# Attention's input x turned by VectorE and moved by DMA; output tiles 2 and 3 re-placed

## What is computed

```python
x = x + jnp.tanh(g_xattn[0]) * _L0_xattn_ref(_layernorm(x, axis=-1), ctx_1024, ctx_1024, mask_BxS2_if1, Wq, bq, ...)
x = x + jnp.tanh(g_ffn[0]) * _L0_ffn_ref(_layernorm(x, axis=-1), W_r, W_k, W_v, mu_r, mu_k)
```

## Time and profile before

| | |
|---|---|
| median of the runs | 1876.82 us |
| the profiled execution | 1877.37 us |
| its span | 1875.6 us, granted clock 0.996 |
| TensorE busy | 1843.8 us, 98% |
| VectorE / ScalarE / GpSimd busy | 1372.9 / 1069.8 / 1142.2 us |
| DMA, mean | 130 GB/s, 243.32 MB |

### The profile page before, as it was taken

One profiled execution on the slowest core, in us unless ns is written; L12 is line 12 of the kernel. 1 busy time (PEld: TensorE's weight loads), 2 busy tenths in 40 slices (PEclk: granted clock), 3 DMA queues, 4 the chain that ended last, 5 costly groups with the idle time before them and its releaser, 6 DMA issues.

```text
span 1875.6 us, 35183 instructions
## 1 busy us (share of the span) xinstructions
PE 1843.8 (98%) x10928; PEld 1449.0 (77%) x10928; DVE 1372.9 (73%) x3732; ACT 1069.8 (57%) x2055; POOL 1142.2 (61%) x1833
## 2 busy tenths in 40 slices
PE   6999999999999999999999999999999999999999
PEld 5677777777777777777777777777678888888887
DVE  6776777677676777677677677767688787888864
ACT  5655555565555556555565555556575555656562
POOL 2777777777677777767777777776652423233231
PEclk9999999999999999999999999999999999999999
DMA  7555465445546545554645556465244535353421
GB/s 220 105 133 129 125 159 122 129 122 143 132 113 163 124 119 127 143 148 100 163 114 124 134 130 156 114 159 141 68 135 124 146 108 162 100 149 112 140 86 68
DMA packets 159801, 243.32 MB, mean 130 GB/s; under 512 B 22752, under 2 KB 51424, under 8 KB 158848
## 3 DMA queue, kind: packets, MB, share of 16 engines
q1 hardware_dynamic: 159616, 241.07, 49.7%
HBM read 92.06 MB, written 33.59 MB: 67 GB/s over the span
## 4 chain that ended last, share of the span: by engine, by line
PE 94%; DVE 3%; issue 1%; DMA 1%; POOL 0%; ACT 0%; SPq 0%; DVEq 0%; ACTq 0%
PE proj_ps L41 15%; PE proj_ps L42 15%; PE proj_ps L43 15%; PE score_ps L1446 10%; PE prob_ps L1470 8%; PE value_ps L1489 8%; PE score_ps L41 3%; PE score_ps L43 3%; PE score_ps L42 3%; PE sum_ps L1497 2%; PE sum_ps L43 1%; PE sum_ps L41 1%; PE sum_ps L42 1%; PE value_ps L41 1%; PE value_ps L43 1%; PE value_ps L42 1%
## 5 line engine op out<-in xcount | busy, mean ns | idle before, releaser
L1089 DVE CUSTOM_DVE_ANT_0 score_ps<-score_ps,causal 128x128 f32<-128x128 f32 (+3 forms) x1024 | 488.8, 505 | 291.5 <-PE score_ps L1446 291.4
L692 ACT ACTIVATE probs<-prob_ps 128x512 f32<-128x512 f32 (+1 forms) x768 | 396.1, 528 | 368.6 <-PE prob_ps L1470 184.6
L1446 PE MATMUL score_ps<-k_stack,q_stack 97*128 97x128 f32 (+3 forms) x1024 | 318.9, 353 | 4.5 <-DVE least L1089 3.6
L1470 PE MATMUL prob_ps<-q_stack,k_stack 100*128 100x512 f32 (+3 forms) x1024 | 280.5, 314 | 2.8 <-DMA q_stack<-max_rows 2.7
L563 POOL TENSOR_TENSOR kact<-square,kact 128x512 fp32r<-128x512 f32 x64 | 96.0, 1510 | 306.3 <-ACT kact L778 306.3
L495 POOL TENSOR_TENSOR prob_sum<-probs 128x384 f32<-128x384 f32 x256 | 260.0, 1016 | 0.0
L1446 PEld LDWEIGHTS score_ps<-k_stack,q_stack 97*128 97x128 f32 x1024 | 187.5, 189 | 75.1 <-issue 39.8
L498 POOL TENSOR_TENSOR prob_sum<-prob_sum,probs 128x256 f32<-128x256 f32 x256 | 198.2, 774 | 37.0 <-POOL prob_sum L495 0.4
L1470 PEld LDWEIGHTS prob_ps<-q_stack,k_stack 100*128 100x128 f32 x1024 | 192.0, 191 | 22.3 <-DMA q_stack<-max_rows 3.3
L484 POOL TENSOR_SCALAR_AFFINE_SELECT probs<-probs 128x256 f32<-128x256 f32 x256 | 104.7, 409 | 152.7 <-ACT probs L692 152.7
L488 POOL TENSOR_SCALAR_AFFINE_SELECT probs<-probs 128x256 f32<-128x256 f32 x256 | 106.8, 417 | 125.1 <-ACT probs L692 125.1
(11 more groups left out here) (180 smaller groups left out, 4665.2 us busy)
## 6 DMA issues: line engine op xcount, KB each, us to landing
k_stack<-staged SPq DMA_DIRECT2D x384, 128.0 KB
q_stack<-staged SPq DMA_DIRECT2D x384, 128.0 KB, 3.1
x_io<-in_x SPq DMA_DIRECT2D x16, 1024.0 KB, 7.9
x<-x_io SPq DMA_DIRECT2D x64, 256.0 KB, 3.1
res<-x SPq DMA_DIRECT2D x64, 256.0 KB, 3.4
out_x<-res SPq DMA_DIRECT2D x64, 256.0 KB, 5.4
tiles<-in_x SPq DMA_DIRECT2D x15, 1024.0 KB, 5.4
tiles<-in_ctxT SPq DMA_DIRECT2D x60, 256.0 KB, 3.9
```

Source lines behind the costliest of these rows:

```text
L692: nc.scalar.activation(probs[:, u % RING, lo:hi], prob_ps[(3 * u + c) % 2][:, 0:hi - lo], ACT.Exp, scale=SCALE).then_inc(exp_done, 1)
L1089: nc.vector.tensor_tensor_reduce(out=here, in0=here, in1=causal[:, LATE - P * t:S], scale=-1.0, scalar=3e38, op0=ALU.add, op1=ALU.min, acc ...
L1446: last = nc.tensor.matmul(here[:, at:at + P * (t + 1)], q_stack[n][0:MASK_ROW + 1, j, P * t:P * t + P], k_stack[n][0:MASK_ROW + 1, j, 0:P ...
L1470: last = nc.tensor.matmul(here[:, at:at + width], k_stack[n][0:ROWS, j, P * k:P * k + P], q_stack[n][0:ROWS, j, P * k:S], start=True, stop ...
```

## The change

For the batches 1 to 15 the x is no longer transposed on TensorE. The new room `turning` holds per tile 128 + 512 columns; `tiles` is its upper 512. Step by step for batch b+1:

- `load_x` makes four DMAs of 32 partitions, so that partition 32a+c, tile m holds token 128a+32m+c.
- `apply_layernorm` writes 128 columns lower, and within each chunk with features regrouped (the write goes in steps of 32 elements).
- Slot 8, between `maximum` 1 and 2, VectorE: four `turn_normalised`, one per chunk, each a transposition in 32x32 blocks of 128x512, each waiting for the one before.
- Slot 9, SyncE: `move_normalised` 0 and 1 ahead of `stack_q`, 2 and 3 behind it, each 256 KB from 32 partitions of `tiles` into all 128 partitions of x_room[1] (the room of xT_low). They wait for the turned tiles and for the last queries of batch b.
- Slots 10 and 11: `high_part_x` and `low_part_x` in their old places, but both now read x_room[1] in SBUF, not a bank.
- xT is kept by quarters of 128 tokens; the queries' moving operand is read as 4 pieces of 128 columns.
- `load_c` waits for the four moves.

Output tiles 2 and 3 start in the first place of slots 10 and 11, one chunk there, two in the second place, one in the third; tile 2 goes to the queries' bank 0. x_io has 3 tiles: tile 2 shares the room of tile 0, so its residual is loaded in slot 8 after tile 0 is stored, and its bias is added by GpSimd in slot 10, not in slot 3. The residual comes in four DMAs. For the last batch tile 2 uses `turning`. The x of the FFN's first batch is still transposed on TensorE in slots 10 and 11 of batch 15, with tiles 0 and 2 now in the keys' bank, so that `x0` waits for `k_low`. `x_blocks` of the FFN moves to another room.

The diff, cut to its changed lines; conditions that keep the old way for batch 0, and semaphores, are left out:

```diff
-        tiles = sb("tiles", [P, T, D])
-        x_io = sb("x_io", [P, T, D])
+        turning = sb("turning", [P, T, P + D])
+        tiles = turning[:, :, P:P + D]
+        x_io = sb("x_io", [P, 3, D])
...
-            10: ("x0+,x1+", "o2- 01", "o2- 23,x2+"),
-            11: ("x3+", "o3- 01", "o3- 23"),
+            10: ("x0+,x1+,o2- 0", "o2- 12", "o2- 3,x2+"),
+            11: ("x3+,o3- 0", "o3- 12", "o3- 3"),
...
-                "q3": 0, "k3": 1, "x0": 0, "x1": 2, "x2": 0, "x3": 2, "o2": 1, "o3": 1}
+                "q3": 0, "k3": 1, "x0": 0, "x1": 2, "x2": 0, "x3": 2, "o2": 0, "o3": 1}
...
-                  "q3": ("o0", -1), "x0": ("q3", -1), "x2": ("x0", 0), "x3": ("x1", 0),
+                  "q3": ("o0", -1), "o2": ("q3", 1), "x0": ("o2", -2), "x2": ("x0", 0), "x3": ("x1", 0),
...
-                  "k3": ("o1", -1), "o2": ("k3", 1), "o3": ("o2", 0)}
+                  "k3": ("o1", -1), "o3": ("k3", 1)}
...
+        def x_bank(b, m):
+            return proj_ps[1] if b == B and m % 2 == 0 else bank(f"x{m}")
...
-                if 0 <= b < B:
+                if 0 <= b < B and (name[0] != "x" or b == 0):
...
-        x_blocks = x_io[:].rearrange("p t d -> p (t d)").rearrange("p (n m c) -> p n m c", m=T, c=SIDE)
+        x_blocks = wo_room[1][:].rearrange("p t d -> p (t d)").rearrange("p (n m c) -> p n m c", m=T, c=SIDE)
...
+        def x_row(b, m):
+            return turning[:, :, 0:P] if (b, m) == (B - 1, 2) else x_io[:, (0, 1, 0, 2)[m], :]
...
+        def as_row(here, b, m):
+            return here.rearrange("p (n c) -> p n c", n=T) if (b, m) == (B - 1, 2) else here
...
+        def quarter(tensor, a):
+            return tensor[:].rearrange("p k n -> p (k n)")[:, K * P * a:K * P * a + K * P]
...
+        def by_quarters(tensor, k):
+            return tensor[:].rearrange("p k n -> p (k n)").rearrange("p (a k n) -> p a k n", a=QUARTERS, k=K)[:, :, k, :]
...
+        def turned_on_tensor(b):
+            return T * (0 if b == 0 else b - B + 1)
...
-                    sp.wait_ge(xt_done, T * b)
+                    sp.wait_ge(xt_done, turned_on_tensor(b))
...
-                    sp.wait_ge(xt_done, T * (b - 1))
+                    sp.wait_ge(xt_done, turned_on_tensor(b - 1))
...
+                elif b < B:
+                    for a in range(QUARTERS):
+                        here = x[b, P * a:P * a + P].rearrange("(m c) d -> c m d", c=SIDE)
+                        sp.dma_start(tiles[SIDE * a:SIDE * a + SIDE], here).then_inc(x_loaded, 16)
...
-                    here = (x[b] if b < B else x1[b - B]).rearrange("(t p) d -> p t d", p=P)
-                    sp.dma_start(tiles[:] if b <= B else x_in[:], here).then_inc(x_loaded, 16)
+                    here = x1[b - B].rearrange("(t p) d -> p t d", p=P)
+                    sp.dma_start(tiles if b <= B else x_in[:], here).then_inc(x_loaded, 16)
...
+            def move_normalised(b, a):
+                sp.wait_ge(ln_turned, K * b)
+                sp.wait_ge(q_done, K * b)
+                sp.dma_start(quarter(x_room[1], a), tiles[SIDE * a:SIDE * a + SIDE]).then_inc(ln_moved[a], 16)
...
-                sp.wait_ge(xt_done, T * b + k + 1)
+                for a in range(QUARTERS):
+                    sp.wait_ge(ln_moved[a], 16 * b)
...
-            def load_residual(b):
-                for m in range(T if b > 0 else 0):
-                    sp.wait_ge(x1_stored[m], 16 * b)
-                sp.dma_start(x_io[:], x[b].rearrange("(t p) d -> p t d", p=P)).then_inc(res_loaded, 16)
+            def load_residual(b, m):
+                if m == 2 and b < B - 1:
+                    sp.wait_ge(x1_stored[0], 16 * (b + 1))
+                elif m == 2:
+                    for n in range(QUARTERS):
+                        sp.wait_ge(ln_moved[n], 16 * (B - 1))
+                elif b > 0:
+                    sp.wait_ge(x1_stored[2 if m == 0 else m], 16 * b)
+                elif m < 2:
+                    sp.wait_ge(mask_stored, 16)
+                sp.dma_start(x_row(b, m), as_row(x[b, P * m:P * m + P], b, m)).then_inc(res_loaded[m], 16)
...
-                sp.dma_start(x1[b, P * m:P * m + P], x_io[:, m, :]).then_inc(x1_stored[m], 16)
+                sp.dma_start(as_row(x1[b, P * m:P * m + P], b, m), x_row(b, m)).then_inc(x1_stored[m], 16)
...
-                    load_residual(b - 1)
+                    for m in (0, 1, 3):
+                        load_residual(b - 1, m)
+                    if b == B:
+                        load_residual(b - 1, 2)
+                if has_prev and s == 8:
+                    load_residual(b - 1, 2)
+                if has_next and s == 9:
+                    move_normalised(b + 1, 0)
+                    move_normalised(b + 1, 1)
...
+                if has_next and s == 9:
+                    move_normalised(b + 1, 2)
+                    move_normalised(b + 1, 3)
...
-                pool.wait_ge(res_loaded, 16 * (b + 1))
-                nc.gpsimd.tensor_tensor(x_io[:, m, :], x_io[:, m, :], bo_gated[:], ALU.add).then_inc(res_ready, 1)
+                pool.wait_ge(res_loaded[m], 16 * (b + 1))
+                nc.gpsimd.tensor_tensor(x_row(b, m), x_row(b, m), as_row(bo_gated[:], b, m), ALU.add).then_inc(res_ready, 1)
...
-                if s in (2, 3) and 0 <= b - 1 < B - 1:
-                    add_residual_bias(b - 1, 2 * (s - 2))
-                    add_residual_bias(b - 1, 2 * (s - 2) + 1)
+                if s == 2 and 0 <= b - 1 < B - 1:
+                    add_residual_bias(b - 1, 0)
+                    add_residual_bias(b - 1, 1)
+                if s == 3 and 0 <= b - 1 < B - 1:
+                    add_residual_bias(b - 1, 3)
+                if s == 10 and 0 <= b - 1 < B - 1:
+                    add_residual_bias(b - 1, 2)
...
-                here = x_tile(b, m)
-                nc.scalar.activation(here, here, ACT.Identity, bias=newton[:, 3, m:m + 1], scale=newton[:, 1, m:m + 1]
+                here = there = x_tile(b, m)
+                if 0 < b < B:
+                    here = here.rearrange("p (k c g) -> p k c g", k=K, g=QUARTERS)
+                    there = turning[:, m, 0:D].rearrange("p (k g c) -> p k c g", k=K, g=QUARTERS)
+                nc.scalar.activation(there, here, ACT.Identity, bias=newton[:, 3, m:m + 1], scale=newton[:, 1, m:m + 1]
...
-                act.wait_ge(xt_done, T * b + m + 1)
-                if b > 0:
+                if b == 0:
+                    act.wait_ge(xt_done, m + 1)
+                    nc.scalar.copy(quarter(xT[0], m), bank(f"x{m}")[:]).then_inc(xt_high, 1)
+                else:
+                    act.wait_ge(ln_moved[m], 16 * b)
...
-                nc.scalar.copy(xT[0][:, :, P * m:P * m + P], bank(f"x{m}")[:].rearrange("p (k n) -> p k n", k=K)
-                               ).then_inc(xt_high, 1)
+                    nc.scalar.copy(quarter(xT[0], m), quarter(x_room[1], m)).then_inc(xt_high, 1)
...
-                act.wait_ge(xt_done, T * (B + j) + m + 1)
+                act.wait_ge(xt_done, turned_on_tensor(B + j) + m + 1)
...
-                here = bank(f"x{m}") if j == 0 else x_ps[m % 2]
+                here = x_bank(B, m) if j == 0 else x_ps[m % 2]
...
-                    for n in range(T):
-                        dve.wait_ge(x1_stored[n], 16 * B)
+                    dve.wait_ge(o_done, T * B)
...
-                nc.vector.tensor_tensor(xT[1][:, :, P * m:P * m + P], bank(f"x{m}")[:].rearrange("p (k n) -> p k n", k=K),
-                                        xT[0][:, :, P * m:P * m + P].bitcast(F32), ALU.subtract).then_inc(xt_low, 1)
+                here = bank(f"x{m}")[:] if b == 0 else quarter(x_room[1], m)
+                nc.vector.tensor_tensor(quarter(xT[1], m), here, quarter(xT[0], m).bitcast(F32), ALU.subtract).then_inc(xt_low, 1)
...
+            def turn_normalised(b, k):
+                dve.wait_ge(ln_applied, T * (b + 1))
+                wait(dve, ln_turned, K * b - 1 - k)
+                nc.vector.transpose(out=tiles[:, :, P * k:P * k + P].rearrange("p g (m c) -> p m g c", c=SIDE),
+                                    in_=turning[:, :, P * k:P * k + P].rearrange("p m (g c) -> p m g c", c=SIDE)
+                                    ).then_inc(ln_turned, 1)
...
-                dve.wait_ge(res_ready, T * b + m + 1)
-                nc.vector.scalar_tensor_tensor(out=x_io[:, m, :], in0=o_bank(b, m)[:], scalar=gate[:, 0:1],
-                                               in1=x_io[:, m, :], op0=ALU.mult, op1=ALU.add).then_inc(o_added, 1)
+                dve.wait_ge(res_ready, T * b + (1, 2, 4, 3)[m])
+                nc.vector.scalar_tensor_tensor(out=x_row(b, m), in0=as_row(o_bank(b, m)[:], b, m), scalar=gate[:, 0:1],
+                                               in1=x_row(b, m), op0=ALU.mult, op1=ALU.add).then_inc(o_added, 1)
...
-                if has_next and s == 11:
+                if has_next and b >= 0 and s == 8:
+                    for k in reversed(range(K)):
+                        turn_normalised(b + 1, k)
```

(19 more changed lines are left out.)

25 lines of the change are left out of this document (14 added, 11 removed).

## The result

The changed kernel takes 1907.43 us (1905.78 to 1915.45), the kernel before beside it 1876.74: a ratio of 1.0173, 95% interval 1.0144 to 1.0202, so 30.7 us slower. The forecast was 1872.3 us, with a range of 1861 to 1885. The profiled execution took 1906.58 us, span 1904.8.

A forecast was written before the change was run, and what follows sets the result against it. The prediction took TensorE to bound the kernel (94% of the chain), with VectorE late next. 15 batches x 0.4 us = 6.0, minus 1.5 once per run, gave 4.5 us off 1876.8: 1872.3 us, range 1861 to 1885.

The forecast's parts named there:

- What TensorE loses: Slots 10 to 12: without the transposes of x TensorE needs 1.7 us less per batch, at most 25.5 us.
- The transpositions: Slot 8, VectorE: four transpositions take 3.0 us, just hidden in 3.07 us of idle time; ScalarE's normalisation priced at 0.
- The low part of x: Slots 10 and 11, VectorE: subtractions with both inputs in SBUF cost 1.07 us more per batch, leaving 0.4 us gain.
- GpSimd: Slot 10: the bias of tile 2 takes 1.27 us, starts after VectorE's first subtraction of x, and costs 0.
- bias goes first: Rival, slot 10: GpSimd's bias starts before VectorE's subtraction, which loses 1.1 us; 8.3 us slower, 1885.1 us; chance 0.22.
- SyncE and the moves: Slots 9 to 11: moves take 1.3 us each; TensorE waits 1.1 us for the maxima rows, at no extra cost.
- Nothing on SyncE is later: Slots 9 and 10: with four moves of some 0.6 us issuing each, the maxima rows still issue at 724.17.
- I take 202 GB/s: Slots 9 and 10: the moves run at the rate of the stack DMAs, 1.3 us each.
- lies beside the other and costs nothing more: Slot 11: TensorE's 1.1 us wait for the maxima rows is covered by VectorE's lateness, adding 0.
- Once per run: Batch 15: `x0` in the keys' bank waits for the low part of k3, 1.5 us lost.
- Only the maxima rows are late: Rival, slot 11: only the wait for these rows remains; 0.6 us gained per batch, 7.5 us faster, 1869.3; chance 0.12.
- turn the next maxima at 732.1: After slot 11's wait for the maxima rows, TensorE alone would do this then; VectorE allows it only at 732.3.

The follow-up runs named there:

- a_tiny9: `a_tiny` with GpSimd's bias of output tile 2 moved from slot 10 to slot 9: 1870.07 us, ratio 0.9962.
- a_tiny: Changed kernel with each move cut to 8 columns per source row, both parts of x read from a constant tile: 1875.27 us, ratio 0.9993.
- a_wide: Changed kernel with each move reading all 128 partitions of one tile, same bytes, features in another order: 1877.51 us, ratio 1.0005.
- c_ports: Changed kernel with the moves issued in the order 0, 2, 1, 3, parts of x in the same order: 1892.03 us, ratio 1.0073.
- a_half: Changed kernel with each move cut to 256 of 512 columns, parts of x read from a constant tile: 1874.2 us, ratio 0.9985.

## Why the prediction was wrong, point by point

- **What TensorE loses: right.** 1.7 us forecast, 1.5 us by the period of `a_tiny9`.
- **The transpositions: right.** Four take 3.16 us (894.17 to 897.33) and the next maximum starts at 897.28; the score that it reads ends only 0.04 us earlier. The normalisation with its scattered write takes 1.33 us and not 0.80. Its price of 0 held, but with nothing to spare: the last of the four ends at 894.14, 1.1 us into slot 8, and the transpositions begin at 894.17.
- **The low part of x: right in kind, too large, and not what decided****.** Mean 0.87 us over all 60, where 0.96 was forecast. In this batch the four are 0.69, 1.17, 0.96 and 0.69:

```profile
906.01 0.69 DVE L1126 TENSOR_TENSOR xT_low<-xT_room_low,xT_high 128x512 fp32r<-128x512 f32 x1 [0.23 <-ACT xT_high L704]
...
907.23 1.17 DVE L1126 TENSOR_TENSOR xT_low<-xT_room_low,xT_high 128x512 fp32r<-128x512 f32 x1
...
911.46 0.57 DVE L1154 CUSTOM_DVE_ANT_0 score_ps<-score_ps,causal 128x384 f32<-128x384 f32 x1 [0.92 <-PE score_ps L1514]
```

  The last row is the point: VectorE, which I took for the engine that is late next, itself waits 0.92 us for a TensorE that stood still. Where the moves carry next to nothing, VectorE's lateness leaves 0.8 us of gain per batch (`a_tiny`, 80.5 us for 81.25), and I had left 0.4.
- **GpSimd: the order as forecast, the time not****.** VectorE's subtraction started at 906.01, 0.01 us ahead of the bias. The bias took 1.83 us in this place and not 1.27. It ended at 907.85; the next subtraction, begun at 907.23, ended at 908.40, 1.17 us long:

```profile
906.02 1.83 POOL L554 TENSOR_TENSOR x_io<-x_io,bo_gated 128x512 f32<-128x512 f32 x1
```

  The rival "bias goes first" did not come about. With the bias in slot 9, `a_tiny9`, the subtractions are 0.18 us shorter in the mean and the bias takes 1.30 us. The exclusion that the Trainium skill states, "SBUF — State Buffer", section "SBUF: two separate sides", is borne out by these numbers.
- **SyncE and the moves: this step failed.** "Nothing on SyncE is later" was wrong by 1.1 us: 0.8 from the stack DMAs' issue (2.63 for 1.83), 0.3 from the two moves, which with the gaps around them take 1.50 us where 1.21 were free. Some 0.4 of it comes with the issues themselves, whatever they carry, for in `a_tiny` the rows are issued 2.27 us after slot 10 begins, for 1.88 before and 2.97 here (medians). "I take 202 GB/s" was too fast: moves 0 and 1 were to be in by 722.8, which in this batch's time is 903.8, and the second landed at 905.9. The landing of the rows at 727.7 was too early with it: in this batch's time that is 908.7, and TensorE got the rows at 910.05, while it wanted them at 907.84 (forecast: 907.6). The wait was 2.2 us and not 1.1. And the sentence that such a wait "lies beside the other and costs nothing more" fell with it: at 2.2 us it sets the batch alone.
- **What was missing: the clock.** No term of the sum allowed for TensorE's granted clock. With waits over 2 us it cost another 10.2 us in the batches 1 to 14, and more in batch 0.
- **Once per run: right for its term.** The wait of `x0` in batch 15 is 1.39 us, where 1.5 was forecast:

```profile
1319.56 0.65 PE L1642 MATMUL proj_ps<-ident,turning 128*128 128x128 f32 x4 [1.39 <-DVE staged L1143]
```

  From slot 8 of batch 15 on the run is 3.0 us longer in all. Another wait, 1.28 us at 1333.41 and not in the kernel before, is for ScalarE's copy of the maxima (line 736), which stands behind a cast of FFN weights (line 783) that waited 1.03 us for its DMA.
- **The rivals.** None was this one. "Only the maxima rows are late" named the wait and priced it at a gain, because it took the rate as given. What had been missing is a rival in which the moves run slower than the stacks, since four of them follow each other from 32 partitions each. The runs settle the cause: 32 source partitions per move (`a_wide`), of which about half is that neighbours share the same half of the partitions (`c_ports`), and a loss that begins above half of the bytes (`a_half`). Of the other half the landings show that a narrow move that follows none of its kind still takes 3.72 us, for 2.32 from 128 partitions. Why a full queue makes SyncE's issues longer stays open.
- **A term of the waiting sum.** The terms named for "turn the next maxima at 732.1" (727.7, the old distance of 4.72, plus 0.2, minus 0.7) give 731.9. The chunk of tile 3 doesn't leave that distance, as it stands behind the probabilities (910.39 after 910.05); what leaves it is x3. The measured distance, 910.05 to 914.42, is 4.37 us.

## What to carry to other kernels

Work taken off the bounding engine and given to DMA needs a sum of its own. Start where the queue is empty, add the bytes at the rate of the side with the fewest partitions, and go on to the first small transfer that somebody waits for. Spread each transfer over all partitions, or at least alternate the halves. Look for the point from which the backlog reaches the small transfer: here half of the bytes cost nothing and all of them 30.7 us. Price an idle time of 2 us or more on TensorE above its length, for in 6 of 14 batches a stretch at half clock came on top.

## What the runs showed of the hardware

- **DMA issue on SyncE is no constant.** Three stack DMAs of 128 KB: 1.83 us before, 2.63 behind two narrow moves, 1.90 with the moves alternating halves, 1.89 behind two wide ones, 4.42 with moves 2 and 3 in ScalarE's queue.
- **Alternating halves of the partitions** in one queue, the parts of x following the same order, gave 15.4 us (1907.4 to 1892.0). The second of two moves lands 4.05 us after its issue in place of 5.17.
- **The clock after a wait.** Granted clock 0.50 for 3.4 us behind idle times of 2.1 to 2.5 us in six batches; not behind all of them: batches 5 and 7 waited 2.03 and 2.77 us and kept the full clock.
- **A scattered write on ScalarE**, 128x512 f32 in steps of 32 elements: 1.33 us, where the same activation in place took 0.80.
